# Loading the input by batch inside the first attention, and storing the output by half batch inside the last stage

## What is computed

```
xn = layer norm(x);  gate = sigmoid(sum |xn|)
q = rotary((xn * gate) @ Wq);  k, v = split(xn @ Wkv);  k = rotary(k)
x = x + softmax(where(mask, q k / 4 - slope * |i - j|, -1e9)) v @ Wo + bo
```

## Time and profile before

| | |
|---|---|
| median of 3 runs | 1861.69 us (1856.41 to 1864.27) |
| span of the profiled execution, from its first to its last instruction | 1867.2 us |
| TensorE busy | 1647.8 us, 88% of the span |
| VectorE, ScalarE, GpSimd busy | 1131.8, 867.8, 470.7 us |
| DMA | 160.30 MB, mean 86 GB/s |

### The profile page before, as it was taken

The page is one execution under the profiler, slowest core; times in us unless marked ns, Lnnn a source line. Parts: engine busy times, 40 slices in busy tenths (PEclk is TensorE's granted clock), DMA queues, the critical chain, the costliest instruction groups (busy, mean ns, idle before and its releaser), DMA issues. The chain is left out here.

```text
span 1867.2 us, 29072 instructions
## 1 busy us (share of the span) xinstructions
PE 1647.8 (88%) x10776; PEld 966.2 (52%) x10782; DVE 1131.8 (61%) x2567; ACT 867.8 (46%) x1358; POOL 470.7 (25%) x593
## 2 busy tenths in 40 slices
PE   4899999899999999954799999779998999998776
PEld 2344444478855666533456656456774344443533
DVE  2687777343245665647667776355454787774476
ACT  1266556533215555532135555447671566665322
POOL 4222120023313322010332230036772522200100
PEclk9799899999999999965899999979999999999699
DMA  7350441100064345000534532211114345320322
GB/s 243 88 142 35 108 119 23 68 1 0 1 175 128 85 120 159 2 9 0 155 93 129 142 114 47 77 52 52 52 52 139 99 105 158 88 71 1 122 91 91
DMA packets 68961, 160.30 MB, mean 86 GB/s; under 512 B 10285, under 2 KB 15926, under 8 KB 67962
## 3 DMA queue, kind: packets, MB, share of 16 engines
q1 hardware_dynamic: 68826, 158.51, 30.0%
HBM read 109.05 MB, written 53.09 MB: 87 GB/s over the span
## 5 line engine op out<-in xcount | busy, mean ns | idle before, releaser
L1078 DVE TENSOR_REDUCE a_mx<-PS 128x1 f32<-128x512 f32 (+3 forms) x768 | 395.0, 553 | 192.6 <-PE PS L1320 128.8
L1261 ACT ACTIVATE a_pT<-PS 128x1024 f32<-128x1024 f32 (+3 forms) x384 | 310.4, 812 | 214.8 <-PE PS L1344 151.7
L1315 PE MATMUL PS<-a_k,a_q 64*128 64x512 f32 (+3 forms) x768 | 231.9, 414 | 10.2 <-DVE a_mx L1078 6.1
L405 DVE CUSTOM_DVE_ANT_0 PS<-PS,a_dist 128x448 f32<-128x448 f32 x256 | 156.4, 644 | 62.9 <-PE PS L650 60.6
L1335 PE MATMUL PS<-a_q,a_k 64*128 64x512 f32 (+3 forms) x768 | 172.5, 435 | 6.8 <-issue 5.0
L1358 PE MATMUL PS<-a_pT,a_va 128*32 128x512 f32 (+3 forms) x1536 | 164.3, 499 | 5.6 <-ACT a_raw L1219 5.4
L555 ACT ACTIVATE a_pT<-PS 128x448 f32<-128x448 f32 (+1 forms) x256 | 124.6, 540 | 92.1 <-PE PS L673 91.8
L122 PE MATMUL PS<-cst 128*128 128x512 f32 x248 | 132.0, 661 | 37.7 <-PEq L66 28.7
L1315 PEld LDWEIGHTS PS<-a_k,a_q 64*128 64x128 f32 x768 | 110.1, 185 | 79.4 <-DVE a_mx L1078 60.7
L1335 PEld LDWEIGHTS PS<-a_q,a_k 64*128 64x128 f32 x768 | 74.9, 184 | 144.1 <-issue 68.5
L2074 POOL TENSOR_TENSOR f_h_low<-f_prod,f_h_high 128x512 fp32r<-128x512 f32 x84 | 111.5, 1334 | 60.8 <-ACT f_h_high L2261 55.6
(11 more groups left out here) (355 smaller groups left out, 3406.4 us busy)
## 6 DMA issues: line engine op xcount, KB each, us to landing
spread_scratch<-a_high SPq DMA_DIRECT2D x96, 256.0 KB, 3.4
a_q<-spread_scratch SPq DMA_DIRECT2D x96, 256.0 KB, 5.5
a_k<-spread_scratch SPq DMA_DIRECT2D x96, 256.0 KB, 6.2
f_gb<-gate_rows SPq DMA_DIRECT2D x68, 256.0 KB, 5.1
spread_scratch<-a_low SPq DMA_DIRECT2D x48, 256.0 KB, 4.1
a_q<-window_scratch SPq DMA_DIRECT2D x32, 256.0 KB, 5.4
a_k<-window_scratch SPq DMA_DIRECT2D x32, 256.0 KB, 6.0
window_scratch<-a_high SPq DMA_DIRECT2D x24, 256.0 KB, 4.7
```

The costliest lines, as they stand in the source:

```text
L405: dve.tensor_tensor_reduce(PS[:, 4 + a, 0:KW], PS[:, 4 + a, 0:KW], dt_[:, off:off + KW], 1.0, 3e38, ALU.add, ALU.min, mx[:, gg % 2, qt, 2 ...
L1078: dve.tensor_reduce(mx[:, gg % 2, qt, 2 * half + a:2 * half + a + 1], PS[:, 4 + a, 0:kw], AX.X, ALU.max).then_inc(max_done, 1)
L1261: act.activation(pT[:, N // 2 % 2, N % 2, :, q0:S], PS[:, 2 * (N % 2):2 * (N % 2) + 2, q0:S], ACT.Exp, scale=SCALE).then_inc(exp_done, 1)
L1315: mm = pe.matmul(ps[:, 0:kw], q[rows, b % 2, pair, qt * P:(qt + 1) * P], k[rows, b % 2, pair, 0:kw], start=True, stop=not causal)
```

## The change

`transfer_in` and `transfer_out` are removed. `attention_window` is given the input, the constants and the scratch copies to do, and `experts` the output.

In the first stage SyncE loads batch 0 of the input first, then `wv`, the first 3 copies to `window_scratch`, `dist`, batch 1, `m`, the masks and the bias; behind the fetches for batch 0 it loads batches 2 and 3, makes the other 3 copies and loads `wo`; behind the fetches for batch 1 it makes the 8 copies to `spread_scratch` for the later stages. ScalarE issues, ahead of its first activation, the constants, `wqk`, `tabs` and `qscale`. VectorE waits for a batch of the input ahead of its statistics, TensorE for the constants ahead of its first transpose. SyncE waits for 3 copies instead of 6 ahead of its first store, and for 6 ahead of the stores of batch 1.

In the last stage SyncE stores each half of a batch when VectorE has added it: of batch b - 1 behind the row fetches of batch b, of the last batch at the end, and waits there for all eight stores. The stage's end with its two meetings then follows.

```diff
 (attention_window, SyncE)
-                sp.dma_start(wqk[:, :, :].rearrange("p a b -> p (a b)"), weights[:, 0:o]).then_inc(loaded_qk, 16)
-                sp.dma_start(tabs[:, :, :].rearrange("p a b -> p (a b)"), rope[:, :]).then_inc(loaded_tab, 16)
-                sp.dma_start(qscale[:, :], scale[:, :]).then_inc(loaded_tab, 16)
+                def load_x(b):
+                    sp.dma_start(X[:, TB * b:TB * b + TB, :], x[b].rearrange("(t p) d -> p t d", p=P)).then_inc(x_in[b], 16)
+
+                def fill_places(par):
+                    for u in range(NU):
+                        sp.dma_start(scr[par, u, 2, :, :, :].rearrange("d l c -> (d l) c"),
+                                     fill[0 if u else 1]).then_inc(filled, 16)
+
+                load_x(0)
                 sp.dma_start(wv[:, :, :].rearrange("p a b -> p (a b)"), weights[:, o:o + KC * VD]).then_inc(loaded_v, 16)
+                fill_places(0)
                 sp.dma_start(dt_[:, :], dist[:, :]).then_inc(loaded_dist, 16)
-                sp.dma_start(masks_in, masks[:, :]).then_inc(loaded_masks, 16)
+                load_x(1)
...
-                sp.wait_ge(filled, 16 * 2 * NU)
+                sp.wait_ge(filled, 16 * NU)
...
                 for b in range(NB):
+                    if b == 1:
+                        sp.wait_ge(filled, 16 * 2 * NU)
                     store_unit(b, 0)
...
                     fetch_group(b, 3)
+                    if b == 0:
+                        load_x(2)
+                        load_x(3)
+                        fill_places(1)
+                        sp.dma_start(wo[:, :, :].rearrange("p a b -> p (a b)"),
+                                     weights[:, o + KC * VD:o + KC * VD + KC * D]).then_inc(loaded_o, 16)
+                    if b == 1:
+                        for par in range(2):
+                            for u in range(4):
+                                sp.dma_start(later_scr[par, u, 2, :, :, :].rearrange("d l c -> (d l) c"),
+                                             later_fill[u % 2]).then_inc(later_filled, 16)
 (VectorE)
+                dve.wait_ge(x_in[0], 16)
                 layer_norm_dve(dve, ln, 0, source(0))
 (ScalarE)
+                act.dma_start(cst[:, :], consts[:, :]).then_inc(loaded_cst, 16)
+                act.dma_start(wqk[:, :, :].rearrange("p a b -> p (a b)"), weights[:, 0:KC * WC]).then_inc(loaded_qk, 16)
+                act.dma_start(tabs[:, :, :].rearrange("p a b -> p (a b)"), rope[:, :]).then_inc(loaded_tab, 16)
+                act.dma_start(qscale[:, :], scale[:, :]).then_inc(loaded_tab, 16)
                 for i in range(KC):
                     keep_turn(0, i, i)
 (experts, SyncE)
+                def store_outputs(b, i):
+                    sp.wait_ge(y_added, TB // 2 * b + i + 1)
+                    k = 2 * i
+                    sp.dma_start(out[b, k * P:(k + 2) * P, :].rearrange("(t p) d -> p t d", p=P),
+                                 X[:, TB * b + k:TB * b + k + 2, :]).then_inc(x_stored, 16)
...
+                    if b:
+                        for i in range(TB // 2):
+                            store_outputs(b - 1, i)
+                for i in range(TB // 2):
+                    store_outputs(NB - 1, i)
+                sp.wait_ge(x_stored, 16 * NB * TB // 2)
 (removed with their calls)
-def transfer_in(nc, X, cst, x, consts, scr, fill, filled, window_scr, window_fill, window_filled):
-            sp.dma_start(cst[:, :], consts[:, :]).then_inc(x_loaded, 16)
-            sp.dma_start(X[:, :, :], x.rearrange("b (t p) d -> p (b t) d", p=P)).then_inc(x_loaded, 16)
...
-            sp.wait_ge(x_loaded, 32)
-def transfer_out(nc, X, out):
-            sp.dma_start(out.rearrange("b (t p) d -> p (b t) d", p=P), X[:, :, :]).then_inc(x_stored, 16)
-            sp.wait_ge(x_stored, 16)
```

More of the change, by code:

```diff
@@ L122, in keep_busy, with attention_window @@
         pe.matmul(PS[:, bank, :], cst[:, C_ID:C_ID + P], cst[:, 0:512], start=True, stop=True)
-def attention_window(nc, tag, X, cst, PS, scr, filled, weights, rope, scale, dist, slopes, masks, preset_m, bias):
+def attention_window(nc, tag, X, cst, PS, scr, filled, weights, rope, scale, dist, slopes, masks, preset_m, bias,
+                     x, consts, fill, later_scr, later_fill, later_filled):
     R32 = mybir.dt.float32r
@@ L169, in attention_window @@
         masks_in = at[:, :, :, :].rearrange("p a b c -> p (a b c)")[:, 0:2 * (P + MW)]
+        x_in = [sem(f"x_in{b}") for b in range(NB)]
+        loaded_cst = sem("loaded_cst")
         loaded_qk, loaded_v, loaded_o = sem("loaded_qk"), sem("loaded_v"), sem("loaded_o")
@@ L246, in _ @@
                 o = KC * WC
[L247 to L249 removed]
+                def load_x(b):
[5 more added lines that the diff above has]
+                load_x(0)
                 sp.dma_start(wv[:, :, :].rearrange("p a b -> p (a b)"), weights[:, o:o + KC * VD]).then_inc(loaded_v, 16)
+                fill_places(0)
                 sp.dma_start(dt_[:, :], dist[:, :]).then_inc(loaded_dist, 16)
[L252 removed]
+                load_x(1)
                 for s in range(2):
                     sp.dma_start(m[:, s, :, :].rearrange("p a b -> p (a b)"), preset_m[:, :]).then_inc(loaded_m, 16)
+                sp.dma_start(masks_in, masks[:, :]).then_inc(loaded_masks, 16)
                 sp.dma_start(bb[:, :], bias.rearrange("(a n) -> a n", a=1).broadcast_to([P, D])).then_inc(loaded_bias, 16)
[L256 to L258 removed]
+                sp.wait_ge(filled, 16 * NU)
                 def store_unit(b, u):
@@ L469, in _ @@
                     exchange(0, u)
+                dve.wait_ge(x_in[1], 16)
                 layer_norm_stats(dve, ln, 1, source(1))
@@ L492, in _ @@
                         if N % STEPS == 23:
+                            dve.wait_ge(x_in[c], 16)
                             layer_norm_stats(dve, ln, c, source(c))
@@ L739, in piece @@
                         outputs(b, i)
+                pe.wait_ge(loaded_cst, 16)
                 for i in range(KC):
@@ L2433, in _, with experts @@
                 pe.wait_ge(o_added, TB // 2 * NB)
-def experts(nc, tag, X, cst, PS, gate_rows, t):
+def experts(nc, tag, X, cst, PS, gate_rows, t, out):
     NU = NE + 1
@@ L2476, in experts @@
         p_done, y_added = sem("p_done"), sem("y_added")
+        x_stored = sem("x_stored")
         def item(g):
@@ L2752, in _ @@
                 pe.wait_ge(y_added, TB // 2 * NB)
-def transfer_in(nc, X, cst, x, consts, scr, fill, filled, window_scr, window_fill, window_filled):
-    with nc.semaphore("x_loaded") as x_loaded, nc.Block() as block:
-        @block.sync
-        def _(sp):
-            sp.dma_start(cst[:, :], consts[:, :]).then_inc(x_loaded, 16)
-            sp.dma_start(X[:, :, :], x.rearrange("b (t p) d -> p (b t) d", p=P)).then_inc(x_loaded, 16)
-            for par in range(2):
-                for u in range(3):
-                    sp.dma_start(window_scr[par, u, 2, :, :, :].rearrange("d l c -> (d l) c"),
-                                 window_fill[0 if u else 1]).then_inc(window_filled, 16)
-            for par in range(2):
-                for u in range(4):
-                    sp.dma_start(scr[par, u, 2, :, :, :].rearrange("d l c -> (d l) c"), fill[u % 2]).then_inc(filled, 16)
-            sp.wait_ge(x_loaded, 32)
-def transfer_out(nc, X, out):
-    with nc.semaphore("x_stored") as x_stored, nc.Block() as block:
-        @block.sync
-        def _(sp):
-            sp.dma_start(out.rearrange("b (t p) d -> p (b t) d", p=P), X[:, :, :]).then_inc(x_stored, 16)
-            sp.wait_ge(x_stored, 16)
 def build(nc, t, out, stages=8):
@@ L2804, in build @@
             latent_experts(nc, "f2", X, cst, PS, gate_rows, t)
-        res = X
         if stages >= 7:
@@ L2808, in build @@
             attention_quads(nc, "a3", X, Y, cst, PS, scr, filled, t["a3_w"], bias=t["a3_bias"], scrambled=True)
-            res = Y
         if stages >= 8:
-            experts(nc, "f3", Y, cst, PS, gate_rows, t)
-        transfer_out(nc, res, out)
+            experts(nc, "f3", Y, cst, PS, gate_rows, t, out)
 def alibi_slopes():
```

4 lines of the change are left out of this document (2 added, 2 removed).

## The result

The changed kernel takes 1845.4 us in the median of 9 runs (1840.28 to 1857.07), against 1860.92 us for the kernel before, run beside it (9 runs, 1854.44 to 1865.64). The ratio is 0.9938, with a 95% interval of 0.9913 to 0.9962: 11.5 us faster (7.1 to 16.2). The ratio is not the quotient of the two medians, which lie 15.5 us apart. The forecast was 13.6 us, 1848.1. Both intervals hold 13.6.

What follows compares the result with a forecast made beforehand. TensorE, busy for 88% of the span, was taken to set the pace, so moved transfers gain only at the two ends: 7.3 + 0.8 + 5.5 = 13.6 us off the median 1861.69 gives 1848.1 us, range 1842 to 1857.

Steps and rivals of the forecast that it cites:

- Batch 0 at 5.7: Front: batch 0 of the input lands at 5.7 us, so the first layer norm starts 7.3 us earlier (3.5 to 9.3).
- The wait for a_wqk, 0.8: Front: TensorE's first projection no longer waits for its weights, which gains 0.8 us.
- First score tile 8 us before 49.03: Sign in the first stage: if the norm starts early but this tile does not come 8 us earlier, the forecast is wrong.
- granted clock in the first 100 us: Sign at the front: the forecast is wrong if TensorE's granted clock there is lower than before.
- What moves further costs nothing: First and last stages: moved loads, copies and stores fit into SyncE's idle time, costing 0 us.
- the hole: Last stage: 15 us in which SyncE had nothing to issue before the last batch's weights; stores fitting there cost nothing.
- The back, 5.5: End of the span: storing the last batch by halves ends it at 1861.7 instead of 1867.2, gaining 5.5 us.
- Rival (a): First score loop: one lower-clock stretch of 4.8 us vanishes (1843.3) or is added (1852.9); chance of one worse 0.10.
- (b): Front: batch 0 lands late, at 9.5 us, and with the store at the median the gain is 8.8 us, 1852.9; chance 0.10.
- (c): First stage: a wait ending at a fixed time swallows the front's shift, leaving only the back, 1856.2 us; chance 0.05.
- (d): First attention: TensorE stays at the lower clock level through much of it, making the kernel slower, 1871 us; chance 0.05.

Runs made afterwards that it cites:

- one-queue run: Constants, wqk, tabs and qscale issued by SyncE behind batch 0 instead of by ScalarE, against the changed kernel: 1844.27 us in one run.
- first profile: The changed kernel's first profiled execution, nothing else changed: span 1838.5 us, against 1867.2 for the kernel before.
- back alone: The kernel before with its loading block kept and only the output stored by half batch: median 1853.1 us, ratio 0.9971 to the kernel before.
- first timing: The changed kernel timed beside the kernel before, 9 runs each: median 1845.4 us against 1860.92, ratio 0.9938.
- second profile: The same changed kernel timed and profiled anew: span 1853.0 us; median of its 7 timed runs 1845.4 us, ratio 0.9903 to the kernel before.
- early products: Five extra products of a tile of ones on TensorE before the first transposes, added to the changed kernel: 1844.25 us in one run.

## Why the prediction was right, step by step

- **Batch 0 at 5.7** (3.7 to 9.5): the norm starts at 5.99 and 5.97, 7.0 us gained for 7.3. The share between two queues was the right picture, and the one-queue run shows both sides of it: 4.87 in one queue, 5.99 shared. The sizes were off both ways, and that they met near 5.7 is in part luck: first in one queue batch 0 was reckoned at 3.7 and came at 4.9, sharing was reckoned at 1.5 us (5.2 less 3.7) and cost 1.1, and 0.5 had been put on top. The rule of the Trainium skill that I had weighed ("DMA: Bandwidth & Descriptors", "Issuing engines are not separate DMA queues") agrees in that transfers from two engines interleave. That a second issuer saves issue time is not the whole of it here: it cost the first transfer 1.1 us.
- **The wait for a_wqk, 0.8**: 0.73. The weights landed at 8.6 and the tables near 11.0, not 6.7 and 9.6. Both were sized too small, and nothing hung on either: the projection began at 13.46, after 7.4 us from the norm as reckoned.
- **First score tile 8 us before 49.03**: 40.04 and 41.02, so 9.0 and 8.0. The difference between the two is TensorE's clock in the products before it: the next eight of the projection took 3.70 us in the first profile, 5.40 in the second and in the profile before. Like with like it is 8.0 from the profile before to the second, and 8.15 from the back alone (tile at 48.19, eight products in 3.70) to the first. With the output in one store, also at 5.40, the tile came at 41.19, 7.8 earlier, so the sign of 8 us was set at the edge of what the clock leaves open. The granted clock in the first 100 us was not lower than before: 0.95 and 0.90 against 0.88.
- **What moves further costs nothing**: SyncE's queue stood for 26.8 us behind the moved transfers, and VectorE waited for X only once, for batch 0. The stores of the second batch are issued from 1792.76 to 1793.74, and the weights of the last one only at 1807.89, well inside the hole (the additions of the earlier trace rows are those of the second batch).
- **The back, 5.5**: 5.6; the span closes 3.5 us after the last addition, where 3.6 was forecast. The 7.5 us of the output store, less a fixed part, priced the half batches well: 256 KB landed in 2.2 us, by the reckoning 2.25. The median of the scratch stores, 3.4, would have been the wrong row.
- **Rival (a), the clock, was priced wrongly.** It had one stretch, 4.8 us, and a chance of 0.10. The same kernel profiled twice differs by 14.5 us through the clock, more than the change is worth. The forecast holds because the mean clock differs from one execution to the next (0.944 to 0.956 in the nine of the first timing) and the median is over many. Judged by two profiles, the change would look twice as large as it is (28.7 us) or, with the second profile (1867.2 to 1853.0, 14.2 us), about as large by luck.
- **Rivals (b), (c), (d)**: batch 0 was not late, the shift reached the end of the stage whole (7.8 to 8.1 for 7.7), and the first attention was not slower.

What stays open is why TensorE's level falls in the first score loop of some executions and not of others. In the three with 0.92 us of waiting or less ahead of the tile it stayed high, and with 2.03 too; with 1.70 it fell, and so it did with the 3.17 to 3.79 of all the others.

## What to carry to other kernels

At the start of a program the path waits for one small piece of the input: load that piece first and alone, and put what is wanted microseconds later behind it, in the same queue if the second queue would only share the engines. Here the one queue was worth a microsecond up to the projection; in the total it was not shown. At the end, what counts is the size of the last store after the last computed value, so store by pieces as they become final. Compare stretches by their milestones, and runs by their granted clock, before a difference of two spans is put down to a change.

## What the runs showed of the hardware that was not expected

TensorE's first work after a start runs at the lower level though the clock column reads 1.00 for it: the four groups of the projection took 3.75 us there and 1.95 behind the early products, and the eight transposes ahead of them, in the same two profiles,

```profile
10.74 1.94 PE L646 MATMUL PS<-cst,a_ln_xn 128*128 128x128 f32 x8 [10.74 <-DVE a_ln_xn L102]
```

```profile
10.52 1.06 PE L646 MATMUL PS<-cst,a_ln_xn 128*128 128x128 f32 x8 [0.17 <-DVE a_ln_xn L102]
```

The clock has no records before 18 us in the profile after the change, and the column shows 1.00 where it has none; the durations tell the level. And two executions differ by 0.8% in a kernel whose instructions do not change (1838.5 and 1853.0); 7.9 us of it were found in the first stage, in TensorE's level, and for the whole 14.5 the mean clocks of 0.956 and 0.945 give 14.1 on the line.
